# A two-layer attention and expert block: row maxima drawn from a queue in pairs, fourteen steps ahead at the turn of the loop

## What is computed

```python
h = _layernorm(x) * (1 + ca) + sa
x = x + ga * attention(h, 16 heads, causal mask)          # "a = 0" in the kernel
h = _layernorm(x) * (1 + cb) + sb
xn = _layernorm(h) * ln_g + ln_b
o = attention(xn, 32 heads, no mask) @ wo + h             # "a = 1" in the kernel
y = gelu(o @ w1[e] + b1[e]) @ w2[e] + b2[e]               # e: one expert for each half batch
x = x + gb * y
# attention: softmax(q k^T / sqrt(d)) v for each head
```

## Time and profile before

| | |
|---|---|
| time, median of 3 runs | 1746.63 us (1745.0 to 1747.63) |
| time of the profiled execution | 1751.3 us |
| its span from first to last instruction | 1749.4 us |
| mean granted TensorE clock | 0.973 of full |
| one turn of the loop | about 201 us of span |
| PE, DVE, ACT, POOL busy | 85%, 67%, 58%, 30% of the span |

### The profile page before, as it was taken

How to read it: one execution, slowest core, us unless ns; L and a number is a source line. 1 busy time by engine, 2 the same in 40 slices (tenths; PEclk the granted TensorE clock), 3 DMA queues, 4 the chain that set the end, 5 groups by cost and what they waited for, 6 DMA issues and landing times.

```text
span 1749.4 us, 30247 instructions
## 1 busy us (share of the span) xinstructions
PE 1495.2 (85%) x10001; PEld 662.9 (38%) x10001; DVE 1166.8 (67%) x2989; ACT 1007.4 (58%) x2096; POOL 528.3 (30%) x1219
## 2 busy tenths in 40 slices
PE   5785789988999889988899889989899887979767
PEld 4333323344333533345333443335333442314315
DVE  6665589646976479755986469763896458775430
ACT  1252567755676457754676456764577555666571
POOL 4232335222433144222443235231352224200100
PEclk9697999999999999999999999999999999989999
DMA  6741334325235233422444333432443241222201
GB/s 190 200 104 39 108 116 125 99 65 140 79 89 137 76 110 119 107 76 82 126 107 120 88 103 94 100 103 76 131 125 98 65 109 50 84 53 60 82 1 60
DMA packets 136742, 170.48 MB, mean 97 GB/s; under 512 B 16968, under 2 KB 102280, under 8 KB 136592
## 3 DMA queue, kind: packets, MB, share of 16 engines
q1 hardware_dynamic: 130704, 164.17, 34.2%
q10 hardware_dynamic: 5888, 4.37, 0.9%
HBM read 110.67 MB, written 56.66 MB: 96 GB/s over the span
## 4 chain that ended last, share of the span: by engine, by line
PE 65%; DVE 17%; ACT 8%; issue 5%; DMA 2%; POOL 1%; SPq 1%; ACTq 0%; POOLq 0%; DVEq 0%
PE bank_out L1228 16%; PE bank_scores L1209 10%; DVE neg_max L1456 8%; PE bank_max L1180 7%; PE bank_side L1315 7%; PE bank_side L1143 6%; ACT probs L1002 5%; PE bank_side L1299 4%; PE bank_side L1153 3%; PE bank_scores L1299 3%; PE bank_side L1237 2%; PE bank_side L1271 2%; PE bank_side L1280 2%; DVE normed L1406 2%; PE bank_side L1118 1%
## 5 line engine op out<-in xcount | busy, mean ns | idle before, releaser
L1002 ACT ACTIVATE probs<-bank_scores 128x512 f32<-128x512 f32 (+3 forms) x1536 | 753.3, 545 | 403.6 <-PE bank_scores L1209 385.7
L1456 DVE TENSOR_REDUCE neg_max<-bank_max 128x1 f32<-128x512 f32 x1024 | 653.6, 683 | 164.8 <-PE bank_max L1180 159.9
L1209 PE MATMUL bank_scores<-q_stack,k_stack 64*128 64x512 bf16 (+3 forms) x2048 | 317.3, 346 | 92.2 <-ACT probs L1002 77.1
L1228 PE MATMUL bank_out<-probs,v_tile 128*9 128x512 f32 (+4 forms) x3072 | 367.7, 551 | 15.6 <-ACT out_raw L1016 12.4
L1180 PE MATMUL bank_max<-k_stack,q_stack 64*128 64x512 bf16 (+3 forms) x2048 | 316.2, 344 | 70.1 <-DVE neg_max L1456 35.9
L1453 DVE CUSTOM_DVE_ANT_0 bank_max<-bank_max,causal 128x384 f32<-128x384 f32 (+3 forms) x512 | 241.9, 515 | 107.6 <-PE bank_max L1180 104.8
L1209 PEld LDWEIGHTS bank_scores<-q_stack,k_stack 64*128 64x128 bf16 x2048 | 85.0, 93 | 365.0 <-issue 343.5
L869 POOL TENSOR_SCALAR_AFFINE_SELECT probs<-probs 128x512 f32<-128x512 f32 x128 | 80.9, 632 | 347.3 <-ACT probs L1002 347.3
L1180 PEld LDWEIGHTS bank_max<-k_stack,q_stack 64*128 64x128 bf16 x2048 | 105.6, 95 | 154.8 <-issue 107.5
L851 POOL CAST max_parts<-max_row 16x128 bf16<-16x128 f32 x96 | 28.4, 296 | 371.1 <-DVE max_row L1467 371.1
L1315 PE MATMUL bank_side<-w_out,hidden_T 128*128 128x256 f32 x512 | 118.8, 385 | 4.8 <-issue 3.7
(11 more groups left out here) (147 smaller groups left out, 1545.6 us busy)
## 6 DMA issues: line engine op xcount, KB each, us to landing
q_stack<-q_parts SPq DMA_DIRECT2D x124, 256.0 KB, 4.3
k_stack<-k_parts SPq DMA_DIRECT2D x122, 192.0 KB, 6.1
w_in<-in_L_ffn_w_dram SPq DMA_DIRECT2D x16, 1024.0 KB, 5.5
w_out<-in_L_ffn_w_dram SPq DMA_DIRECT2D x16, 1024.0 KB, 8.3
q_parts<-partsq SPq DMA_DIRECT2D x32, 384.0 KB, 2.6
k_parts<-partsk SPq DMA_DIRECT2D x32, 384.0 KB, 2.8
q_parts<-partsq SPq DMA_DIRECT2D x32, 256.0 KB, 2.9
k_parts<-partsk SPq DMA_DIRECT2D x32, 256.0 KB, 3.1
```

The source lines that it names most:

```text
L1002: nc.scalar.activation(probs[s % 2][:, head_at(k), q0:S], region[bank][:, q0:S], ACT.Exp, scale=float(WIDTH[a]) ** -0.5).then_inc(drained[ ...
L1209: ins = pe.matmul(region[to][:, q0:S], k_stack[buf][rows, at, kt * P:(kt + 1) * P], q_stack[buf][rows, at, q0:S], start=(i == 0), stop=last)
L1228: ins = pe.matmul(outb[32 * k:32 * k + WIDTH[a] + 1, q0:S], v_tile[a][:, kt, g * GROUP + k, :], probs[s % 2][:, k, q0:S], start=(kt == 0), ...
L1456: v.tensor_reduce(dst, region[bank], AX_X, ALU.max).then_inc(drained[bank], 1)
```

## The change

Maxima are no longer tied to the step that is a fixed lead ahead. They form one queue of pairs (two slots each), and the function `attention` takes from it as many as the list `counts` says for each half step. Items `("maxima_pair",)` in `beside` take one more. Four things follow from the numbers given:

- In the five later turns twelve half steps take no pair (`skipped`): those of p = 1, 2, 3, 6, 8, 9, 10, 13, 18, 19 and 21, most of which have norms, features or projections beside them. In `after` nine half steps of p = 1 to 13 take none.
- The experts take twelve pairs more in every turn: one after each piece of the first product, and between and behind the pieces of the second.
- The lead at the turn is 14 steps where it was 8. The first turn begins with 8 and ends with 14, so it skips nothing and is now a section of its own, `turn0`; `loop` has five turns. `after` has twelve pairs fewer to do.
- In `after`, `load_gate` and the last batch's expert loads move from slot 176 to 186, and `bias_part` from 184 to 200.

The item max_rows follows its group's last pair by three half steps, with a step more where it would meet a normalise, and so moves with the queue.

```diff
+LOOP_LEAD = 14
...
+    def maxima_pair(half):
+
+        (off, a, s), part = pairs.pop(0)
+        out.extend(("maxima", off, a, s, k) for k in range(2 * part, 2 * part + 2))
+        if part == 1 and s % GROUP == GROUP - 1:
+            p = (half + rows_gap + 1) // 2
+            later((p + (p % T_STEPS == NORMALISE_STEP), TURN_SLOT), ("max_rows", off, a, s // GROUP))
...
-            elif steps:
-                out += [("maxima", *steps[0], k) for k in half if k not in early]
...
+            for _ in range(counts[2 * p + h] if 2 * p + h < len(counts) else 0):
+                maxima_pair(2 * p + h)
...
-        for n in range(2):
+        for n in range(4):
             items += [*in_pieces("expert_in", off, j, n), ("gelu", off, j, n)]
-
-        items += [("values_early",), ("maxima_early", 0), ("maxima_early", 1)]
-        for n in range(2, 4):
-            items += [*in_pieces("expert_in", off, j, n), ("gelu", off, j, n)]
-        items += [("maxima_early", 2), ("maxima_early", 3)]
+            items += [("values_early",), ("maxima_pair",)] if n == 1 else [("maxima_pair",)]
...
-        place_at(plan, (start + 2, start + 2 * SLOTS), [("expert_out", off, j, k) for k in range(2)])
+        first, second = (in_pieces("expert_out", off, j, k) for k in range(2))
+        place(plan, start + 2, [*first[:2], ("maxima_pair",), *first[2:], ("maxima_pair",)], 0)
+        place(plan, start + 2 * SLOTS, [*second[:2], ("maxima_pair",), *second[2:]], 0)
...
+    skipped = {(1, 1), (2, 1), (3, 1), (6, 0), (8, 0), (9, 0), (10, 0), (13, 0), (13, 1), (18, 0), (19, 0), (21, 1)}
+    after_experts = {(at, 0) for at in experts_at}
...
-    place(beside, n1 + 48, [("load_gate", 1), ("load_expert_in", 1, 0), ("load_expert_out", 1, 0)])
-    place(beside, n1 + 56, [("bias_part", 1, 0), ("bias_columns", 1)])
+    place(beside, n1 + 58, [("load_gate", 1), ("load_expert_in", 1, 0), ("load_expert_out", 1, 0)])
+    place(beside, n1 + 72, [("bias_part", 1, 0), ("bias_columns", 1)])
```

More of the change, by code:

```diff
@@ L80, in in_pieces, with pairs_of, attention @@
     return [(*item, part) for part in range(PIECES[item[0]])]
-def one_each(steps):
-    return [(step,) for step in steps]
-def attention(main, lead, beside, handed=(), hand_on=None, rows_after=(ROWS_AFTER, ROWS_AFTER), sooner={}):
-    out, waiting = [], {}
+def pairs_of(steps):
+    return [(step, half) for step in steps for half in range(2)]
+def attention(main, pairs, counts, beside, handed=(), hand_on=None, rows_gap=2, sooner={}):
+    out, waiting, pairs = [], {}, list(pairs)
     for at, item in handed:
@@ L110, in attention @@
                     out.append(("scores", *main[p], k))
-            if len(steps) == 2:
-                out += [("maxima", *steps[h], k) for k in range(GROUP)]
-            elif steps:
-                out += [("maxima", *steps[0], k) for k in half if k not in early]
-            early.difference_update(half)
+            for _ in range(counts[2 * p + h] if 2 * p + h < len(counts) else 0):
+                maxima_pair(2 * p + h)
             ready = [item for k in half for item in waiting.pop((p, k), [])]
@@ L134, in attention @@
             off, a, s = main[p]
-            if "values" in early:
-                early.discard("values")
-            else:
+            if not early:
                 later((p + 1, VALUES_SLOT[a]), ("values", *main[p]))
+            early = False
             if s % T_STEPS == T_STEPS - 1:
@@ L142, in attention @@
                 later((p + NORMALISE_AFTER, TURN_SLOT), ("normalise", off, a, s // T_STEPS))
-        for off, a, s in steps:
-            if s % GROUP == GROUP - 1:
-                later((p + rows_after[a], TURN_SLOT), ("max_rows", off, a, s // GROUP))
+    assert not pairs
     for p, k in sorted(waiting):
@@ L152, in attention @@
         assert slot >= count * SLOTS
-        out += [item for item in beside[slot] if not item[0].endswith("_early")]
+        out += [item for item in beside[slot]]
     return out
@@ L159, in turn_on, with all_but @@
     return sorted((at, (i[0], i[1] - 1, *i[2:])) for at, i in handed)
+def all_but(steps, skipped):
+    return [0 if (half // 2, half % 2) in skipped else 1 for half in range(2 * steps)]
 def place(plan, at, items, every=1):
@@ L335, in sections @@
     place_experts(beside, 0, n1 + 15)
-    place(beside, n1 + 48, [("load_gate", 1), ("load_expert_in", 1, 0), ("load_expert_out", 1, 0)])
-    place(beside, n1 + 56, [("bias_part", 1, 0), ("bias_columns", 1)])
+    place(beside, n1 + 58, [("load_gate", 1), ("load_expert_in", 1, 0), ("load_expert_out", 1, 0)])
+    place(beside, n1 + 72, [("bias_part", 1, 0), ("bias_columns", 1)])
     place_experts(beside, 1, 2 * n1 + 3)
-    ahead = steps_of_attention(0, 1)[LEAD:] + steps_of_attention(1, 1)
-    after = attention(steps_of_attention(0, 1) + steps_of_attention(1, 1), one_each(ahead), beside, handed)
+    for slot in beside:
+        if slot >= 2 * n1:
+            beside[slot] = [item for item in beside[slot] if item not in (("maxima_pair",), ("values_early",))]
+    ahead = pairs_of(steps_of_attention(0, 1)[LOOP_LEAD:] + steps_of_attention(1, 1))
+    skipped = {(1, 1), (2, 1), (3, 1), (6, 0), (7, 0), (9, 0), (10, 1), (12, 1), (13, 0)} | after_experts
+    counts = all_but(2 * steps, skipped)
+    given = sum(item == ("maxima_pair",) for slot in beside for item in beside[slot])
+    while sum(counts) > len(ahead) - given:
+        counts.pop()
+    after = attention(steps_of_attention(0, 1) + steps_of_attention(1, 1), ahead, counts, beside, handed)
     after = [item for item in after if item != ("keep_x", 2)]
-    return (("start", start), ("scale", scale), ("first", first), ("second", second), ("before", before), ("loop", loop), ("after", after))
+    return (("start", start), ("scale", scale), ("first", first), ("second", second), ("before", before), ("turn0", turn0), ("loop", loop), ("after", after))
 EARLY_NAMES = ("first", "second", "before")
@@ L391, in number_fills @@
                 count[bank] += 1
-        turns = (LOOPS if name == "loop" else 1)
+        turns = LOOPS - 1 if name == "loop" else 1
         if name == "loop":
@@ L559, in build @@
         y_stored = [sem("y_stored%d" % j) for j in range(2)]
-        main_names = ("before", "loop", "after")
+        main_names = ("before", "turn0", "loop", "after")
         def number(fill):
@@ L585, in walk @@
                              if i[0] not in PIECES or i[-1] == PIECES[i[0]] - 1]
-                for turn in range(LOOPS if name == "loop" else 1):
+                first = {"loop": 1, "after": LOOPS}.get(name, 0)
+                for turn in range(LOOPS - 1 if name == "loop" else 1):
                     for item in items:
@@ L589, in walk @@
                             fs = [(bank, turn * per_loop[bank] + n) for bank, n in filled_by(name, item)]
-                            share[item[0]](item[1] + turn + (LOOPS if name == "after" else 0), fs, *item[2:])
+                            share[item[0]](item[1] + first + turn, fs, *item[2:])
         def previous(a, b):
```

137 lines of the change are left out of this document (72 added, 65 removed).

## The result

The changed kernel takes 1826.56 us (median; 1824.6 to 1828.15), the kernel before 1747.13 us beside it (1745.0 to 1757.42): a ratio of 1.0442, 95% interval 1.04 to 1.0484. Slower was forecast, but 1782 us, with 1802 as the upper end.

A forecast was written before the change was run, and what follows sets the result against it. PE was taken as the bound, busy 1495.2 of 1749.4 us. Five later turns at +9.7 (48.5), `turn0` +3.3 and `after` -16.2 gave +35.6 us on 1751.3; less 4.7 to the median, 1782 us, range 1745 to 1802.

The forecast's parts named there:

- The stack: At p = 3 of later turns PE waits for unit 4's k_stack loads, passing the maxima 10.4 us later; bounds 4.5 and 12.5.
- estimate of 440.6: Clock time in the second turn when the stack would land at the skill page's 341 GB/s, the kernel ending near 1745.
- The clock: Behind the stack's wait in each later turn the granted clock halves, costing 1.8 us; bounds 0 and 3.
- 1.8 us after each such wait: Half of 3.67 us PE busy at half clock, read behind a 7.22 us wait at 1650.33, charged to each later turn.
- Skipped pairs and DVE waits: Per later turn, ten skipped pairs save 2.3 us of PE and DVE's relief 3.5 of 4.0 us of waits.
- Experts: Twelve added pairs at 0.23 us, 2.8 us, plus slower stretches: 3.3 us longer per turn; bounds 1.9 and 5.
- `turn0`: First turn, skipping nothing and using its stack at p = 8 as before: only the experts' 3.3 us longer.
- `after`: Last section 16.2 us shorter, from fewer pairs, fewer DVE waits and a removed long wait, against 3.3 us more in the experts.
- The wait of the earlier trace: The 7.22 us wait at 1650.33 in the last section goes but for 0.3, winning 6.9 us.
- the pairs that p = 48 on no longer holds: In the last section, fifteen pairs gone from p = 48 to 55 save 3.4 us.
- The stack is in time: Rival: PE never waits at p = 3, each later turn 3.5 us shorter, kernel 1716 us; chance 0.12.
- Worse: Rival: experts cost 5 us, DVE waits mostly stay, the stack lands at 449; 72 us longer, 1818 us; chance 0.1.

The follow-up runs named there:

- e4: The changed kernel with nine extra matmuls per later turn ahead of the wait for unit 4's stack, overwritten by the maxima; 1817.42 us, ratio 1.0398.
- e1: The changed kernel with unit 4's stack issued ahead of x_in, w_in and w_out at the loop's turn; 1789.7 us, ratio 1.0242.
- e2: The changed kernel with load_gate and the next x_in, w_in and w_out issued at p = 46, only the stack staying at the turn; 1796.61 us, ratio 1.0278.
- e7: The changed kernel with lead 11, six pairs skipped, the experts' six added pairs between pieces of the first product, none in the second; 1753.78 us, ratio 1.0049.
- e12: As e11, but the two moved pairs stand behind the first piece of the experts' first product; 1737.76 us, ratio 0.9947.
- e11: Kernel before with later last-section loads; two pairs a turn moved from p = 9, 13 to p = 40, 44, every max_rows kept in place; 1736.82 us, ratio 0.994.
- e6: The changed kernel with lead 11, six pairs skipped, the experts' six added pairs within or behind the second product's pieces; 1757.96 us, ratio 1.0059.
- e10: Kernel before with later last-section loads, plus one overwritten fp32 product at p = 23 of the later turns and last section; 1752.06 us, ratio 1.0029.
- e5: Kernel before with later last-section loads; in later turns the second-half pairs of p = 1, 2, 3 taken at p = 11, 16, 17; 1841.31 us, ratio 1.0545.
- e3: The kernel before with only the last section's loads moved later, as in the change; 1740.03 us, ratio 0.9958.

## Why the prediction was right in direction and wrong in size

**The stack.** The mechanism held as written: maxima at p = 3, the loads behind the max_rows of p = 47, and a wait in each later turn but none in `turn0`. PE gets past the maxima 9.9 us later against the turn's start (20.70 against 10.76); the forecast was 10.4. The wait itself was 8.87 us and not some 11 (7.7 to 9.5 in the five turns), mostly because PE came to it 2.1 us later than reckoned, 11.8 us behind the first exponential for 9.8. The 3840 KB from `gb_bc` to the last k_stack took 18.05 us from first issue to last landing, 218 GB/s on average. The Trainium skill's 341 GB/s ("DMA: Bandwidth & Descriptors", section "Bandwidth") is not reached on this average, though it is passed while the loads fill the DMA engines (last column):

```profile
439.00:443.00 4.00, 3.00 (x20) 1.26 (x12) 2.37 (x7) 1.79 (x4) 3.47 (x6) 0.83 1.02 391
```

The prediction's estimate of 440.6 from that page of the Trainium skill fits all 3840 KB (11.5 us from 428.9) and not the 3.5 MB that it names; it changes no term of the sum.

**The clock.** The step "1.8 us after each such wait" failed in size, by a factor of two. From the end of the first later turn's wait to p = 5 the steps took 12.8 us (7.63 and 5.15) where they had taken 8.4 (4.19 and 4.22): 4.4 us, for the half clock stayed 9.4 us after the resumption and not 3.7. In the five turns it stayed 9.4, 9.8, 8.8, 6.6 and 3.6 us and cost 4.4, 4.5, 4.1, 3.1 and 2.0, 3.6 on average; only the last of them is near the length that was taken. e4 shows that PE's idle time keeps the clock down. The rule of the Trainium skill cited ahead, half of the throttled time lost and again in each pass ("TensorE: Matmul & The Clock Gate", section "HAM oscillation — how this bites in real kernels"), agrees: half of 9.4 is 4.7, and it came back in all five turns. What failed was the length taken from one wait of another section; why it differs from turn to turn is open. The fall ahead of the wait cost nothing in this kernel, since PE would only have waited longer; in e1 and e2, where hardly a wait is left to hide it, it is part of the loss, though its share was not measured apart.

**Skipped pairs and DVE waits.** "Most of its 4.0 us of waits should go. I take 3.5" was too much: PE's idle time in p = 5 to 23 fell by 1.1, near the lower bound of 1 that the prediction had reasoned out. PE's busy time fell by 2.95 us, for nine pairs and the two max_rows that left these steps with them. Together 4.0 where 5.8 was forecast (3.7 on average of the five turns; the second of them met the half clock at p = 7). DVE was as forecast, 15.85 of 20 us behind the start of p = 5 (under 16); PE's waits for it were not near zero but 2.4 us.

**Experts.** "12 x 0.23 = 2.8 ... I take 3.3" was low: 5.6 us in each of the six turns. In the whole kernel this step failed by the most. The 0.23 us is the spacing of two 64-row bf16 pairs next to each other; between two fp32 products a pair costs 0.41 by start times and 0.5 in the step's length (e7, e12). Only in ACT's wait at p = 40 and 44 is it free (e7, e11): 4.19 us with one pair and without. Three pairs at p = 40 make it 4.92 (e6).

Of the first later turn's +15.9 us (forecast 9.7), the clock is off by + 2.6, the early part by + 1.8, the experts by + 2.3 and the stack by - 0.5. Of the mean later turn's +15.5 us it is + 1.8, + 2.1, + 2.3 and - 0.4.

**`turn0`** was + 4.2 for 3.3: + 5.6 in the experts, and 1.4 less at p = 0 to 3, where the kernel before had met the half clock and the changed one did not. **`after`** was - 5.3 for - 16.2. The wait of the earlier trace rows went as forecast, and p = 4 to 38 won 8.4 us, near the 9.5 of their terms. Missed were the experts (+ 7.4 us for 3.3, with a wait of 0.7 for a k_stack among them), 2.1 us at p = 0 to 3, where the clock fell with no wait for the stack (0.3), 3.0 us at the end, and the pairs that p = 48 on no longer holds, which won 1.6 us for 3.4. The span grew by 76.8 us for the 35.6 of the sum. Of the 41 us between, the experts' price makes up 18 (2.3 in each of six turns, 4.1 in the last section), skipped pairs and DVE waits 10, the clock behind the wait 9, and the last section's other terms 7; the stack (- 2) and `turn0`'s clock (- 1.4) go against them. A last difference lies in the step from span to time: the median lay 1.6 below the profiled execution (1828.15) in place of 4.7.

**The rivals.** "The stack is in time" promised 1716 us; e1 removes the wait in three of five later turns, shortens it to 2.6 and 1.8 us in the others, and takes 1789.7. The rival's sum lacked the same three things: the clock at the turn, the experts' price, and DVE waits that stay. "Worse" had 1818 us. Two of its terms are close to what was measured, 5 us for the experts (5.6) and 1 us of DVE waits won (1.1); but its later landing did not come (12.1 us behind the old time, measured 8.7 to 10.7), and the clock and the last section made up for it. That the time came so near is in part luck.

**Open.** Whether p = 1 falls to the half clock depends on more than the order of a turn (e10; e5, one turn of five). That it is the time at which a turn begins fits e3, e10 and e12 and was forecast for e10, but nothing else was varied to exclude another cause. In the changed kernel a stretch at half clock begins in p = 1 of all five later turns, 3.6 to 6.2 us behind the first exponential; why in all five was not separated from chance by a run.

## What to carry to other kernels

A queue of look-ahead work is tied to what its end releases: moving pairs also moves the rows, DMAs and loads behind them, and most losses here came from those, not from the pairs. Move the work and hold its followers in place (e11), and put it where the engine already waits, counting the room: one pair in each of ACT's waits was free, three pairs in the step were not. Where an engine is 85% busy, price a change by the idle time that ends and not by the other engine's load: 10 us off DVE gave PE 1.1 us. And where a stretch of thin work meets the half clock in some passes and not in others, compare several passes, begun at different times, before a gain of a microsecond a pass is believed.

## What the runs showed of the hardware

- The granted clock fell to 0.50 with no long wait of PE: at p = 1 in two of the six turns of e10, whose instructions are the same up to p = 22, for 3.4 us each, at a cost of 1.1 and 1.4 us in p = 1 and 2. In a turn of the kernel before in which it did not fall, PE was busy for 2.65 of the 4.45 us of p = 1.
- Behind an idle stretch of 8.87 us the half clock stayed for 9.4 us although PE was busy in 8.93 of 9.5 us; behind idle stretches of 7.7 to 9.5 us in the other turns, for 3.6 to 9.8. With the stretch filled (e4, 1.64 us idle) it came once in five turns, for 3.4 us.
- A 64-row bf16 pair costs 0.23 us beside its like, and 0.41 to 0.52 us between two 128x256 fp32 products.
